# Small-head attentions: weighting two steps behind, between the first and the second score tile

## What is computed

```python
# cross-attention of layer 0 (self-attention of layer 1 likewise, keys from x)
qh = _split_heads(q @ wq.T + bq, b)
kh = _split_heads(k @ wk.T + bk, b)
vh = _split_heads(v @ wv.T + bv, b)
logits = jnp.einsum('bhqd,bhkd->bhqk', qh, kh) * inv_sqrt_depth
weights = jax.nn.softmax(logits, axis=-1)
out = jnp.einsum('bhqk,bhkd->bhqd', weights, vh)
out = out.transpose(0, 2, 1, 3).reshape(b, -1, D_MODEL)
return out @ wo.T + bo
```

## Time and profile before

| | us |
|---|---|
| median of 3 executions | 5171.99 |
| lowest, highest | 5162.75, 5172.54 |
| profiled execution | 5170.67 |
| its span, first to last instruction | 5168.9 |
| TensorE, VectorE, ScalarE busy over the span | 4819.4, 3646.1, 2882.4 |
| mean granted TensorE clock | 0.970 |

### The profile page before, as it was taken

The page is one execution under the profiler, slowest core; times in us unless marked ns, Lnnn a source line. Parts: engine busy times, 40 slices in busy tenths (PEclk is TensorE's granted clock), DMA queues, the critical chain, the costliest instruction groups (busy, mean ns, idle before and its releaser), DMA issues. The chain is left out here.

```text
span 5168.9 us, 71148 instructions
## 1 busy us (share of the span) xinstructions
PE 4819.4 (93%) x23995; PEld 2642.8 (51%) x24010; DVE 3646.1 (71%) x6559; ACT 2882.4 (56%) x6256; POOL 2638.7 (51%) x1567
## 2 busy tenths in 40 slices
PE   6899997899999897899879999999999999999976
PEld 5555555344444587444545555555555555555533
DVE  8677776788888587788646666666666666666658
ACT  5666663477777643577534545444444445454457
POOL 5555554100000251530157777777787877777740
PEclk9999998899999899899989999999999999999989
DMA  6577668432222005332543334343333333343300
GB/s 218 198 241 245 239 241 236 121 82 76 67 76 72 1 1 204 112 93 82 184 118 86 93 83 98 78 102 78 98 83 89 90 86 94 82 101 75 90 17 29
DMA packets 344186, 576.28 MB, mean 111 GB/s; under 512 B 49120, under 2 KB 142368, under 8 KB 342800
## 3 DMA queue, kind: packets, MB, share of 16 engines
q1 hardware_dynamic: 341616, 567.53, 38.3%
q10 hardware_dynamic: 2208, 4.20, 0.2%
HBM read 335.54 MB, written 201.85 MB: 104 GB/s over the span
## 5 line engine op out<-in xcount | busy, mean ns | idle before, releaser
L3005 POOL TENSOR_TENSOR la_acc<-la_acc,la_pr 128x1024 f32<-128x1024 f32 x704 | 1697.4, 2411 | 495.2 <-ACT la_pr L2964 459.9
L2964 ACT ACTIVATE la_pr<-la_s_ps 128x512 f32<-128x512 f32 x1536 | 793.8, 603 | 973.5 <-PE la_s_ps L2813 971.4
L2820 PE MATMUL la_o_ps<-la_pr,lw_vf 128*64 128x512 f32 x3072 | 743.8, 605 | 0.0
L2812 PE MATMUL la_s_ps<-la_q_hl,lw_k_hh 128*128 128x512 f32 x1536 | 691.6, 450 | 1.8 <-ACT la_q_hs L2940 1.4
L1909 DVE TENSOR_REDUCE ca_mx<-ca_m_ps 128x2 f32<-128x1024 f32 x512 | 600.8, 1217 | 118.2 <-PE ca_m_ps L1769 118.2
L1871 ACT ACTIVATE ca_pr<-ca_s_ps 128x512 f32<-128x512 f32 x1024 | 541.9, 601 | 208.3 <-PE ca_s_ps L1776 205.0
L3026 DVE TENSOR_REDUCE la_mx<-la_m_ps 128x2 f32<-128x1024 f32 x384 | 463.1, 1206 | 212.0 <-PE la_m_ps L2795 203.2
L2813 PE MATMUL la_s_ps<-la_q_hs,lw_k_l 65*128 65x512 f32 x1536 | 608.9, 396 | 0.0
L3026 DVE TENSOR_REDUCE la_mx<-la_misc 128x2 f32<-128x1024 f32 x384 | 466.1, 1214 | 1.3 <-PE la_misc L2795 1.3
L2812 PEld LDWEIGHTS la_s_ps<-la_q_hl,lw_k_hh 128*128 128x128 f32 x1536 | 290.0, 189 | 243.5 <-ACT la_pr L2964 103.8
L2820 PEld LDWEIGHTS la_o_ps<-la_pr,lw_vf 128*64 128x64 f32 x3072 | 186.3, 136 | 347.0 <-issue 227.7
(11 more groups left out here) (414 smaller groups left out, 8884.5 us busy)
## 6 DMA issues: line engine op xcount, KB each, us to landing
lw_k_hh<-scratch_k_high SPq DMA_DIRECT2D x128, 512.0 KB, 6.5
scratch_k_high<-sc_k_high SPq DMA_DIRECT2D x128, 256.0 KB, 2.6
scratch_k_low<-sc_k_low SPq DMA_DIRECT2D x128, 256.0 KB, 2.8
lw_w_parts<-scratch_w_parts SPq DMA_DIRECT2D x64, 512.0 KB, 6.2
lw_k_l<-scratch_k_low SPq DMA_DIRECT2D x64, 512.0 KB, 8.4
lw_vf<-scratch_xv SPq DMA_DIRECT2D x64, 512.0 KB, 4.1
cl_ks<-scratch_k_rows SPq DMA_DIRECT2D x384, 64.0 KB, 2.8
scratch_vaug<-sc_v SPq DMA_DIRECT2D x16, 1024.0 KB, 4.4
```

Of the source, the lines that this page charges most:

```text
L2812: pe.matmul(s_ps[:, bank, :], k_hh[:, par, h, keys], q_hl[:, par, h, :], start=True, stop=False)
L2820: last = pe.matmul(o_ps[XD * h:XD * h + XD, :], vf[:, par, st, XD * h:XD * h + XD], pr[:, st % LAG, h, :], start=(st == 0), stop=(st == XT ...
L2964: act.activation(pr[:, st % LAG, h, :], s_ps[:, (2 * st + h) % 3, :], ACT.Exp, scale=scale).then_inc(p_done, 1)
L3005: pool.tensor_tensor(total, total, exps, ALU.add).then_inc(acc_done, 1)
```

## The change

`weigh` is called with the number of the step and runs two steps behind instead of one (LAG). It moves from behind the fourth score tile to between the first and the second. `pr` gets three slots of four tiles (SLOTS), and ScalarE waits before the first exponential of a step until W of three steps earlier is done. The early pairs and the turn, turn back or projection stand after the third tile instead of the second, and the late pairs follow them directly, ahead of the fourth; pairs behind stand after the fourth tile, and so ahead of the next step's first tile and its W. The case of `pairs_of` that put the second pair of steps 0 and 2 of `ca` behind is removed; those pairs are late ones now. ScalarE's `keep_output` moves behind the first exponential of step 1, `keep_back` behind the third of its step. VectorE's and GpSimd's programs are the same but for the order of the bank turns.

```diff
+    LAG, SLOTS = 2, 3
@@ pairs_of
         if PAIRS[kt] == 1:
             return [], pairs, []
-        if PAIRS[kt] == 2 and kt in (OUT, TURN):
-            return pairs[0:1], [], pairs[1:2]
         return pairs[0:1], pairs[1:2], pairs[2:]
@@ the order of bank turns
-                if h == 1:
+                if h == 2:
                     for j in early:
                         m_turns.add("max", j)
@@ tiles
-        pr = pool_.sb("pr", [P, 4, 2, T])
+        pr = pool_.sb("pr", [P, SLOTS, 2, 2, T])
@@ TensorE
-                def weigh(unit, u, kt):
+                def weigh(step):
+                    unit, kt = step // KT, step % KT
+                    u = unit % GROUPS
                     if kt == 0:
                         pe.wait_ge(ot_done, unit)
                         pe.wait_ge(values_loaded[u], VALUE_LOADS * (unit // GROUPS + 1))
-                    pe.wait_ge(p_done, GH * (unit * KT + kt + 1))
+                    pe.wait_ge(p_done, GH * (step + 1))
...
                         early, late, behind = pairs_of(unit, kt)
+                        step = unit * KT + kt
                         scores(unit, u, kt, 0)
+                        if step >= LAG:
+                            weigh(step - LAG)
                         scores(unit, u, kt, 1)
+                        scores(unit, u, kt, 2)
                         for j in early:
                             max_pair(j)
                         for kind, n in after(unit, kt):
...
-                        scores(unit, u, kt, 2)
                         for j in late:
                             max_pair(j)
                         scores(unit, u, kt, 3)
-                        if kt > 0:
-                            weigh(unit, u, kt - 1)
-                        elif unit > 0:
-                            weigh(unit - 1, (u - 1) % GROUPS, KT - 1)
                         for j in behind:
                             max_pair(j)
-                weigh(UNITS - 1, GROUPS - 1, KT - 1)
+                for step in range(UNITS * KT - LAG, UNITS * KT):
+                    weigh(step)
@@ ScalarE
-                        if kt == 1 and unit > 0:
+                        if unit * KT + kt >= SLOTS:
+                            act.wait_ge(pv_done, unit * KT + kt - SLOTS + 1)
+                        weight(unit, kt, 0)
+                        if kt == LAG - 1 and unit > 0:
                             keep_output(unit - 1)
-                        if unit * KT + kt > 1:
-                            act.wait_ge(pv_done, unit * KT + kt - 1)
-                        weight(unit, kt, 0)
                         weight(unit, kt, 1)
+                        weight(unit, kt, 2)
                         for kind, n in after(unit, kt):
                             if kind == "back":
                                 keep_back(n)
-                        weight(unit, kt, 2)
                         weight(unit, kt, 3)
```

More of the change, by code:

```diff
@@ L1782, in weigh @@
                         pe.wait_ge(values_loaded[u], VALUE_LOADS * (unit // GROUPS + 1))
-                    pe.wait_ge(p_done, GH * (unit * KT + kt + 1))
+                    pe.wait_ge(p_done, GH * (step + 1))
                     for h in range(GH):
-                        last = pe.matmul(o_ps[32 * h:32 * h + 32, :], vs[:, u, kt, h, :], pr[:, 2 * (kt % 2) + h // 2, h % 2, :],
+                        last = pe.matmul(o_ps[32 * h:32 * h + 32, :], vs[:, u, kt, h, :], pr[:, step % SLOTS, h // 2, h % 2, :],
                                          start=(kt == 0), stop=(kt == KT - 1))
@@ L1870, in weight @@
                     act.wait_ge(s_ready, n + 1)
-                    act.activation(pr[:, 2 * (kt % 2) + h // 2, h % 2, :], s_ps[:, s_turns.bank("tile", n), :], ACT.Exp,
+                    act.activation(pr[:, (unit * KT + kt) % SLOTS, h // 2, h % 2, :], s_ps[:, s_turns.bank("tile", n), :], ACT.Exp,
                                    scale=scale).then_inc(p_done, 1)
```

## The result

| | before | after |
|---|---|---|
| median of 13 executions each, in turn on the same chip, us | 5171.99 | 5182.86 |
| lowest, highest | 5155.74, 5178.55 | 5171.57, 5187.56 |
| profiled execution, its span | 5170.67, 5168.9 | 5174.83, 5173.0 |
| mean granted TensorE clock in it | 0.970 | 0.968 |

The ratio is 1.0017, with a 95% interval of 1.0010 to 1.0024: 10.9 us more by the medians, where +11.0 was forecast. The interval lies almost wholly within the 0.2% which the prediction took as the measurement's limit. The total agrees better than its parts do, as the rows show.

The account below looks back on a forecast made before the run. The prediction took a closed loop of waits (tile, exponential, bank, tile, weighting) as the bound, with no engine at its limit. Its terms, 0 - 2.7 + 11.8 + 1.9 + 0 = +11.0 us, gave 5183 us against the median, range 5170 to 5197.

Parts of the forecast that it names:

- The bound and the loop: Quiet steps: closed loop of tile, exponential, bank, tile, weighting, 2.67 us before and after; change costs 0.
- lag two: Weighting's new place: costs nothing and is needed, since 1.68 us after S1 the previous step's fourth exponential would be unfinished.
- The quiet step's first term: Quiet step: from score tile to the start of its exponential, 0.59 us, carried over unchanged.
- quiet steps that differ from 2.67: Sign of being wrong: such steps would mean the loop is not the one followed.
- The held step: A max pair waiting ahead of the next first tile and weighting makes a step 3.83 us, 1.16 over a quiet one.
- the 40 us forecast: Sign of being right: TensorE's waits for maxima grow by some 40 us in self-attention.
- The waits for exponentials: Sign of being right: TensorE's waits for exponentials shrink; no size given.
- The first four units of `ca`: Cross-attention units without projection: 22.82 us against 23.50 before, 4 x -0.68 = -2.7 us.
- The clock in `aa`: Rival: clock falls in self-attention, 1.5 us per step; a tenth of the 128 steps gives +19 us; chance 0.03.
- A window of `aa` below 1.00: Sign of being wrong: granted clock under 1.00 in self-attention, where it was to stay 1.00.
- The first rival: Holds overstated or hidden, time within 0.2%: 0 to +10 us, 5172 to 5182; chance 0.34 together with the last rival.
- One price among the rivals: Rival of a faster kernel, held pairs released early: self-attention -1.3 us per unit, about -70 us in all; chance 0.10.

Follow-up runs that it names:

- e8: The changed kernel with the weighting one step behind and two slots, its new place kept: 5546.2 us, 1.0713 against the kernel before.
- e4: The changed kernel with the third max pair of a self-attention step behind the next step's weighting: 5160.48 us, 0.9972 against the kernel before.
- e7: The kernel before with the max pairs behind the weighting moved ahead of it, still behind the fourth tile: 5162.59 us, 0.9985.
- e6: The kernel before with three slots of weighted tiles and nothing else: 5173.87 us, 1.0008.
- e2: The changed kernel with the slot wait written again ahead of each step's second exponential: 5191.98 us, 1.0032 against the kernel before.
- e3: The kernel before with three slots and the slot wait moved ahead of the fourth exponential of the step before: 5158.81 us, 0.9968.
- e1: The changed kernel timed again, unaltered, against the kernel before: 5178.85 us, 1.0009.
- e11: The changed kernel once more with a profile, for the clock alone: one execution, 5183.14 us.
- e5: The changed kernel with self-attention max pairs spread 2, 2, 2, 2 instead of 1, 3, 1, 3: 5152.06 us, 0.9965 against the kernel before.
- e9: The kernel before with pairs ahead of the weighting, 2, 2, 2, 2 in self-attention, three slots and moved slot wait: 5132.04 us, 0.9918.

## Why the prediction was right, and where it wasn't

**The bound and the loop: right.** The first view that told something was the timeline of one step. The loop of the earlier trace rows was found again in every kernel with W two steps behind or behind the fourth tile; only in e8 does W's own wait take the place of the bank. e4 and e7 show that it is the pairs' place that matters and not W's. That the third slot brings nothing is shown by e6, that lag two is needed in this place by e8: the fourth exponential wasn't ready, as the prediction had it for lag one.

**The quiet step's first term: mis-sized.** The prediction took 0.59 from the earlier trace rows and carried it over to "S1, 0.59, its exponential". But in before the exponential on the loop is the step's first, which has the wait for W as well as the one for its tile; after the change it is the second, which has one wait. It measured 0.54. "The same four durations from the earlier trace rows, the same instructions" was the step that failed. The prediction named "quiet steps that differ from 2.67" as what would show the loop wrong. The loop was right, and one instruction less stood on it, as e2 and e3 show from both sides. Over a `ca` unit that makes 23.74 and not 23.98, -6.1 us in all. The last quiet step of a unit didn't gain: it stays at 2.67, since the next unit's first tile starts 0.74 after the exponential and not 0.65. That tile has a second wait of its own, for the shift rows; no run takes it away, so that this is its price isn't shown.

**The held step: right.** 3.83 was forecast, 3.85 came. Its six terms, read off rows of three different steps, were each within 0.01. In `ca` steps 0 and 2 take 3.85, step 1 2.69 (2.71 forecast), step 3 of even units 3.09 (3.19 forecast; 0.06 of that is the shorter first term, for with the wait put back, in e2, it takes 3.15). In `aa` the steps are 3.27, 3.85, 2.80 and 3.85, forecast 3.27, 3.83, 2.84 and 3.83: 13.77 in even and odd units. That it fits to the hundredth is luck in part. The forecast's own terms for step 2, 1.03 + 0.47 + 0.31 + 1.00, make 2.81 and not 2.84, and the slip of 0.03 stands in for the 0.02 that each hold lacks. The waits of weight loads for maxima in `aa` went from 43.8 to 60.4 us, and a row of matmuls with 33.7 is new: they grew, but the 40 us forecast can't be checked on rows that overlap. The waits for exponentials, which were to shrink, didn't: those of the tiles' weight loads went from 143.8 to 189.7 us in `ca` (1100 to 1700) and from 80.5 to 84.0 in `aa`. S3's wait left the path, but the next S0 waits in its place.

**The first four units of `ca`: right in sign, mis-sized.** -0.68 each was forecast, -1.07 came, with the shorter first term in their quiet steps as well.

**The clock in `aa`: a rival that came true in small.** It was given 0.03 and priced at 1.5 us per step for a tenth of the steps, +19. "A window of `aa` below 1.00" was one of the signs of being wrong, and it came. What came was 2.9 us per stretch of about two steps: three stretches in the first profiled execution of the changed kernel, one in e1, five in e11 (the early one cost 5.3), so 3 to 17 us. e2, whose `aa` units are the same, has four. In the trace of before a hold of 1.06 stands in a stretch at 1.00, but one hold per unit isn't two. The holds' number and length don't explain it either: e5 has two of 3.85 in each unit and no stretch. What the profiles do show is that among settled units only those of 13.77 us are hit: all four such executions have stretches, and none of the eight with units of 13.53 us or less has any (each was granted 1.00 from 2120 to 2480). e8's settled units are longer still (15.37), with a lower busy share (294.16 / 359 = 0.82 against 162.55 / 180 = 0.90), and have one stretch near their start and none from 2541 on. Why is open.

**The sum.** Total +11.0 forecast, +10.9 measured, and that closeness is luck. Two errors cancel in it: 6 to 8 us too few won in `ca` (the second wait), and 3 to 17 us too few lost in `aa` (the clock). At equal clock the settled and first units make -6.1 - 4.2 + 11.8 + 2 = +3.5 us. The three executions of the changed kernel with mean clocks of 0.968 to 0.969 took 5171.57 to 5174.83 us, the ten at 0.965 to 0.967 took 5180.89 to 5187.56. It would fit that the number of half-clock stretches in `aa` decides between them, but it isn't shown: only one of the thirteen has a trace, and the kernel before, whose trace has no stretch in settled `aa` units, spreads as widely with the mean clock (5162.47 us at 0.972 to 5182.38 at 0.966 beside e1). The first rival (within 0.2%) was nearly as good a forecast as the one chosen, for a reason it hadn't given. One price among the rivals doesn't add up: with `aa` steps 1 and 3 at 2.7, a unit would be 3.27 + 2.7 + 2.84 + 2.7 = 11.5 us, 1.8 under before and not 1.3. Nothing measured hangs on it.

## What to carry to other kernels

When a queue runs in order, ask of each instruction that can wait what stands behind it, and put it where the other engines already have their next work: with its max pairs ahead of W alone, the kernel (e7, e9) beat both the one that had them behind W and the one that had them ahead of the next tile, though in `aa`, with pairs 1, 3, 1, 3, behind W was 0.23 us per unit better. When a loop of waits is measured, list not only its instructions but each instruction's waits: a wait long fulfilled cost nothing off the loop (e2's held steps, still 3.85) and 0.05 to 0.06 us on it. Ask of a lag or a further slot whether the loop waits for the weighted tile or for the bank: the slot alone left the quiet step at 2.67 (e6), and lag two was needed where W with lag one waits 0.42 us for the weighted tile (e8).

## What the runs showed of the hardware

- An exponential with two waits starts 0.59 us after the tile pair it waits for, one with a single wait 0.53 to 0.54, though the second wait is long fulfilled; the added semaphore instruction shows as 17 ns (before and e6 against e3, e2 against after).
- In settled `aa` units of after, e1, e2 and e11 the granted clock dropped from 1.00 to 0.50 for 6.8 us at a time, 3, 1, 4 and 4 times, and the unit lasted 2.9 us longer each time (after: TensorE's busy share ahead of the first such drop was 0.90).
- With lag one 950 us of a stage were granted 0.72, though the full-clock steps at 1451 to 1461 show TensorE idle ahead of W for only 0.4 to 0.8 us each. Of the 376 us lost, some 275 are more than the waits had been priced at; some 30 of them are `aa`'s longer units at the full clock, 32 x 1.6 us against the 20 priced.
